# The last graph's elu on VectorE, and SyncE's flag load ahead of its waits, in a four-layer graph-attention kernel

## The chip, the cores and the metric

The kernel runs on one NeuronCore of one Trainium2 chip. The metric is the device time of one execution in microseconds (us), lower being better.

## What is computed

32 graphs of 256 nodes with 128 features pass through four residual layers, each on the rectified layer norm of x: a graph attention (0), an attention with four kinds of edges (1), a relational convolution (2), and a second graph attention whose output goes through an elu (3).

```python
h = jnp.maximum(_layernorm(x, axis=-1), 0.0)
x = x + _L0_gnn_ref(h, adj, L0_gnn_W, L0_gnn_a)
h = jnp.maximum(_layernorm(x, axis=-1), 0.0)
x = x + _L1_gnn_ref(h, adj, L1_gnn_a0, L1_gnn_a1, L1_gnn_a2, L1_gnn_a3)
h = jnp.maximum(_layernorm(x, axis=-1), 0.0)
x = x + _L2_gnn_ref(h, L2_gnn_adj, adj, L2_gnn_weight, L2_gnn_bias)
h = jnp.maximum(_layernorm(x, axis=-1), 0.0)
x = x + _L3_gnn_ref(h, adj, L3_gnn_W, L3_gnn_a)   # _L3_gnn_ref ends in jax.nn.elu(h_prime)
```

## The kernel before

The work is cut into 128 units, a layer of a graph each. `ORDER` lists them: layers 0 to 3 for the first 16 graphs, then for the other 16. A graph's 256 nodes lie as 2 x 128 on the partitions, so one tile of x is 128x256 f32. Each engine has its own hand-written program: `pipeline` steps through the units, and at each step calls a list of stages, each with its lag in units, so the list's order and the lags fix the order on each engine. Engines meet at semaphores alone.

What matters here is the end of layer 3 of the last graphs (g = 29, 30 and 31). TensorE puts numerators and sums in a bank (`put_o`). VectorE inverts the sums (`invert_sums`, L709 and L711). ScalarE (`elu_parts`, L566 and L567) makes for each half of the nodes exp(y) into `expy` and relu(y) into `relu_y`, four activations of 128x128 a graph, with the division in their `scale`. VectorE (`elu`, L735) makes min(exp, 1) + relu, which is elu + 1; the 1 was taken out of x before, through `bias_less_1`. Then x is added into `result`: by VectorE for odd graphs (`add_x`, L744), by GpSimd for even ones (`add_x_even`, L405). SyncE stores each result (L325), strictly in the order of the graphs.

Behind the last unit VectorE and TensorE reduce a flag (L756, L760, L1011, L762): it is over zero when the inputs are outside of what the fast path can compute, and then a general path in a loop recomputes everything. With these inputs it is zero. Every engine waits for the flag, loads it into a register and branches over the general path's code (L332 on SyncE, L416, L579, L766, L1034 on the others). The block ends with a meeting of all engines (L111): each drains, GpSimd gathers the signals and lets all go. SyncE alone waits before its flag load for all eight `stored` semaphores (L329).

Of the kernel before, what the change touches and what calls it, by code (L numbers as in the profile page):

```python
# [8 lines left out]
B, N, D = 32, 256, 128  # L9
P = 128  # L10
T = N // P
# [12 lines left out]


SLOTS = 8
BEHIND = 2
EARLY = 3
HS = 12
XS = 12  # L30
WIDE = 16
ROUNDS = B // SLOTS

ALL, ATTEND, GATS, NORMED, MULTI_REL, RGCN_REL = (0, 1, 2, 3), (0, 1, 3), (0, 3), (1, 2), (1,), (2,)
NOT_LAST, FIRST, LAST = (0, 1, 2), (0,), (3,)
# [14 lines left out]
def nth(layers, n):  # L50

    return COUNTS[layers][n]
# [21 lines left out]
def gat_slot(n):  # L74

    return (nth(GATS, n) - 1) % SLOTS

# [22 lines left out]
def gat_stack(nc, x, adj, w0, a0, m0, m1, m2, m3, w2, b2, w3, a3, out):  # L100
    f32, bf16, i32, u32 = mybir.dt.float32, mybir.dt.bfloat16, mybir.dt.int32, mybir.dt.uint32
    ALU = mybir.AluOpType
    ACT = mybir.ActivationFunctionType
# [7 lines left out]
    with ctx:  # L111
# [3 lines left out]
        def sem(name):  # L115
            return ctx.enter_context(nc.semaphore(name))
# [18 lines left out]
        x1 = sb("x1", [P, WIDE, T, D])  # L135
        edges = sb("edges", [P, SLOTS, T, N], i32)
        absent = sb("absent", [P, WIDE, T, N], bf16)

        h = sb("h", [P, HS, T, 1 + D])
        xb = sb("xb", [P, SLOTS, T, D])  # L140
        result = sb("result", [P, SLOTS, T, D])
        st = sb("st", [P, WIDE, T, 9])
# [4 lines left out]
        rinv = sb("rinv", [P, WIDE, T])  # L147

        hT = sb("hT", [P, 4, N])
        haT = sb("haT", [P, 4, N])  # L150
        val = sb("val", [P, SLOTS, T, D + 3])
        edgesT = sb("edgesT", [P, WIDE, T, N])
# [5 lines left out]
        relu_y = sb("relu_y", [P, 4, T, D])  # L158
        expy = sb("expy", [P, 4, T, D])
# [59 lines left out]
        def bank_o(n):  # L219
            return bank[O_BANK[n]][:, 0:T * (1 + D)].rearrange("p (t c) -> p t c", t=T)  # L220
# [4 lines left out]
        stored = [sem(f"stored{k}") for k in range(SLOTS)]  # L225
# [32 lines left out]
        sums_ready = sem("sums_ready")  # L258
        rinv_ready = sem("rinv_ready")
        elu_ready = sem("elu_ready")  # L260
        o_taken = sem("o_taken")
        xb_ready = sem("xb_ready")
        bias_ready = sem("bias_ready")
        result_ready = [sem("result_ready_even"), sem("result_ready_odd")]
# [28 lines left out]
        @block.sync  # L293
        def _(sp):

            def load_first(k):
                sp.dma_start(edges[:, k].rearrange("p t n -> p (t n)"), adj_v[k]).then_inc(edges_loaded[k], 16)

            for k in range(XS):
                sp.dma_start(xin[:, k].rearrange("p t d -> p (t d)"), x_v[k]).then_inc(x_loaded[k], 16)  # L300
                if 2 <= k <= SLOTS + 1:
                    load_first(k - 2)
                if k == 6:
                    sp.dma_start(w_gat[1][:, 0:D], w3).then_inc(gat_loaded[1], 16)
                    sp.dma_start(a_rows[1][:, :], a3.rearrange("(c p) o -> c (p o)", c=2)).then_inc(gat_loaded[1], 16)
            for r, m in enumerate((m0, m1, m2, m3)):
                sp.dma_start(a_rel[:, r:r + 1], m.rearrange("(p o) -> p o", o=1)).then_inc(loaded, 16)
            sp.dma_start(w_rel[:, :, :], w2.rearrange("r i o -> i r o")).then_inc(loaded, 16)
            sp.dma_start(bias[:, :], b2.rearrange("(o d) -> o d", o=1).to_broadcast([P, D])).then_inc(loaded, 16)

            def load_x(n, layer, g):
                if g + XS < B:
                    sp.wait_ge(o_taken, nth(NOT_LAST, n))
                    sp.dma_start(xin[:, g % XS].rearrange("p t d -> p (t d)"), x_v[g + XS]).then_inc(x_loaded[g % XS], 16)

            def load_edges(n, layer, g):
                k = g % SLOTS
                if g + SLOTS < B:
                    sp.wait_ge(absent_ready, nth(FIRST, n))
                    sp.dma_start(edges[:, k].rearrange("p t n -> p (t n)"), adj_v[g + SLOTS]).then_inc(edges_loaded[k], 16)  # L320

            def store(n, layer, g):
                k = g % SLOTS
                sp.wait_ge(result_ready[g % 2], (nth(LAST, n) + 1) // 2)
                sp.dma_start(out_v[g], result[:, k].rearrange("p t d -> p (t d)")).then_inc(stored[k], 16)  # L325

            pipeline([(load_x, SP_LAG, FIRST), (load_edges, SP_LAG, FIRST), (store, SP_LAG + 1, LAST)])
            for k in range(SLOTS):
                sp.wait_ge(stored[k], 16 * ROUNDS)  # L329

            sp.wait_ge(flag_ready, 1)
            with sp.If(sp.value_load(flag[0:1, 0:1], min_val=0, max_val=P) > 0):  # L332
                sp.sem_inc(g_step, 1)
                sp.sem_inc(g_stored, 16)
                with sp.Fori(0, B) as g:

                    sp.wait_ge(g_step, g * G + 1)
                    sp.dma_start(gx[:, :, :].rearrange("p t d -> p (t d)"), x_v[bass.ds(g, 1), :, :].rearrange("o p n -> (o p) n")).then_inc(g_loaded, 16)
                    sp.dma_start(gadj[:, :, :].rearrange("p t n -> p (t n)"), adj_v[bass.ds(g, 1), :, :].rearrange("o p n -> (o p) n")).then_inc(g_loaded, 16)
                    sp.wait_ge(g_step, g * G + G + 1)  # L340
                    sp.dma_start(out_v[bass.ds(g, 1), :, :].rearrange("o p n -> (o p) n"), gout[:, :, :].rearrange("p t d -> p (t d)")).then_inc(g_stored, 16)
                sp.wait_ge(g_stored, 16 * B + 16)

        @block.gpsimd
        def _(pool):
# [52 lines left out]

            def add_x_even(n, layer, g):
                k = g % SLOTS  # L400
                if g % 2 == 0:
                    pool.wait_ge(elu_ready, nth(LAST, n))
                    if g >= SLOTS:
                        pool.wait_ge(stored[k], 16 * (g // SLOTS))
                    pool.tensor_tensor(result[:, k], expy[:, (nth(LAST, n) - 1) % 4], x1[:, g % WIDE], ALU.add).then_inc(result_ready[0], 1)  # L405
# [21 lines left out]
        def _(act):  # L427
# [131 lines left out]
            def elu_parts(n, layer, g):  # L559
                k = g % SLOTS  # L560

                act.wait_ge(rinv_ready, nth(ATTEND, n))
                if nth(LAST, n) > 4:
                    act.wait_ge(result_ready[g % 2], (nth(LAST, n) - 3) // 2)
                for t in range(T):
                    act.activation(expy[:, (nth(LAST, n) - 1) % 4, t], bank_o(n)[:, t, 0:D], ACT.Exp, scale=rinv[:, n % WIDE, t:t + 1])  # L566
                    last = act.activation(relu_y[:, (nth(LAST, n) - 1) % 4, t], bank_o(n)[:, t, 0:D], ACT.Relu, scale=rinv[:, n % WIDE, t:t + 1])  # L567
                last.then_inc(y_ready, 1)

            pipeline([(upper_part, 6, MULTI_REL), (scale_v, 6, LAST), (take_hT, 4, FIRST),  # L570
# [29 lines left out]
        def _(dve):  # L600
# [130 lines left out]
            def elu(n, layer, g):  # L731
                k = g % SLOTS

                dve.wait_ge(y_ready, nth(LAST, n))
                dve.scalar_tensor_tensor(expy[:, (nth(LAST, n) - 1) % 4], expy[:, (nth(LAST, n) - 1) % 4], 1.0, relu_y[:, (nth(LAST, n) - 1) % 4], ALU.min,  # L735
                                         ALU.add).then_inc(elu_ready, 1)

            def add_x(n, layer, g):
                k = g % SLOTS
                if g % 2 == 1:  # L740
                    dve.wait_ge(elu_ready, nth(LAST, n))
                    if g >= SLOTS:
                        dve.wait_ge(stored[k], 16 * (g // SLOTS))
                    dve.tensor_tensor(result[:, k], expy[:, (nth(LAST, n) - 1) % 4], x1[:, g % WIDE], ALU.add).then_inc(result_ready[1], 1)  # L744
# [21 lines left out]
            with dve.If(dve.value_load(flag[0:1, 0:1], min_val=0, max_val=P) > 0):  # L766
                with dve.Fori(0, B) as g:
# [6 lines left out]
                    for t in range(T):  # L774
                        last = dve.tensor_scalar(cols(gabsent, t), adj_t[:, t], 0.0, -BIG, ALU.is_le, ALU.mult)
                    last.then_inc(g_step, 1)
                    for t in range(T):
                        last = dve.tensor_scalar(cols(grel, t), adj_t[:, t], 0.0, float(R + 1), ALU.max, ALU.min)
# [6 lines left out]
                    for layer in range(4):  # L785
                        turn(g, f"{layer}stats")
                        for t in range(T):
                            last = dve.bn_stats(gst[:, t, :], gx[:, t, :])
# [3 lines left out]
                        for t in range(T):  # L792
                            last = dve.bn_aggr(gmv[:, t, :], gst[:, t, :])
                        last.then_inc(g_step, 1)
                        turn(g, f"{layer}norm")
                        for t in range(T):
                            last = dve.tensor_scalar(gxn[:, t, :], gx[:, t, :], gmv[:, t, 0:1], grs[:, t:t + 1],
                                                     ALU.subtract, ALU.mult)
# [14 lines left out]
                        if layer == 2:  # L813
# [5 lines left out]
                            for t in range(T):  # L819
                                last = dve.tensor_tensor(gxb[:, t, :], gx[:, t, :], bias[:, :], ALU.add)  # L820
# [3 lines left out]
                        else:  # L824
# [4 lines left out]
                            for t in range(T):  # L829
                                last = dve.scalar_tensor_tensor(gx[:, t, :], ps_o[:, t, :], grinv[:, t:t + 1],  # L830
                                                                gx[:, t, :], ALU.mult, ALU.add)
# [3 lines left out]
                    for t in range(T):  # L835
                        last = dve.tensor_scalar(gy[:, t, :], ps_o[:, t, :], grinv[:, t:t + 1], None, ALU.mult)
# [267 lines left out]
```

## Time and profile before

| | |
|---|---|
| median of 3 runs | 287.89 us (287.56 to 288.56) |
| the profiled execution's own time | 288.05 us |
| its span, first to last instruction | 285.8 us |
| outside the span | 2.25 us |
| busy: TensorE, ScalarE, VectorE, GpSimd | 274.3, 255.0, 251.9, 234.1 us |
| granted TensorE clock over the span | 0.997 |

The busy times are averages over the whole execution. For a change at the very end the last ten microseconds count: which engine waits for which there, and who comes last to the meeting.

### The profile page before, as it was taken

The numbers are of one execution on the slowest core, as the hardware profiler recorded it, in microseconds if no ns is written. First come the engines' busy times: TensorE is split into PE (matmuls) and PEld (weight loads), VectorE is DVE, ScalarE is ACT, GpSimd is POOL, SyncE is SP. The second block draws the span as 40 slices with busy tenths as digits, with TensorE's granted clock in tenths as the row PEclk, the third lists the DMA queues.
The fourth block names the chain that finished last, engine by engine and source line by source line (L and its number), as shares of the span: only waits on it lengthen the run. The fifth ranks groups of instructions, "written<-read, shape, count | busy, mean of one in ns | idle before, by whom it ended". The sixth has DMA issues, their size and how long they took to land.

```text
span 285.8 us, 8113 instructions
## 1 busy us (share of the span) xinstructions
PE 274.3 (96%) x2252; PEld 257.9 (90%) x2252; DVE 251.9 (88%) x1217; ACT 255.0 (89%) x850; POOL 234.1 (82%) x376
## 2 busy tenths in 40 slices
PE   3999999999999999999999999999999999998991
PEld 2999998888889999999999999888889999998991
DVE  4889999988878887899999999998898888799985
ACT  5998988799998888999999999799999889796994
POOL 4998787777747999999999988887755899999722
PEclk9999999999999999999999999999999999999998
DMA  6946645400000000015333201000000000001213
GB/s 216 319 127 179 177 142 147 167 2 2 0 0 3 0 2 2 3 37 150 98 109 114 73 22 41 18 18 2 1 2 1 3 0 0 3 3 54 76 58 115
DMA packets 15414, 17.79 MB, mean 62 GB/s; under 512 B 2180, under 2 KB 11272, under 8 KB 15368
## 3 DMA queue, kind: packets, MB, share of 16 engines
q1 hardware_dynamic: 15220, 17.18, 19.9%
q8 instruction: 20, 0.33, 0.5%
q14 instruction: 26, 0.21, 0.3%
q10 hardware_dynamic: 148, 0.07, 0.1%
HBM read 13.05 MB, written 4.19 MB: 60 GB/s over the span
## 4 chain that ended last, share of the span: by engine, by line
PE 87%; DVE 8%; ACT 2%; issue 1%; POOL 0%; DVEq 0%; POOLq 0%
PE bank L1001 26%; PE bank L943 10%; PE bank L919 9%; PE bank L948 9%; PE bank L877 7%; PE bank L986 5%; PE bank L956 5%; PE bank L968 5%; PE bank L998 4%; PE bank L903 3%; PE bank L950 2%; DVE pT L699 2%; DVE expy L735 1%; PE bank L922 1%; DVE st L624 1%
## 5 line engine op out<-in xcount | busy, mean ns | idle before, releaser
L367 POOL TENSOR_TENSOR rs<-mv,minus_half 128x2 f32<-128x2 f32 x128 | 89.8, 702 | 35.5 <-DVE mv L635 35.0
L1001 PE MATMUL bank<-val,pT 128*128 128x129 f32 x512 | 74.6, 275 | 0.0
L1001 PEld LDWEIGHTS bank<-val,pT 128*128 128x128 f32 x512 | 67.3, 192 | 0.0
L384 POOL TENSOR_TENSOR h<-h,rs 128x256 f32<-128x256 f32 x93 | 58.2, 626 | 2.3
L699 DVE SCALAR_TENSOR_TENSOR pT<-bank,val,edgesT 128x256 f32<-128x256 f32 x128 | 55.0, 471 | 0.8 <-PE bank L956 0.7
L624 DVE BATCH_NORM_STATS2 st<-x 128x6 f32<-128x128 f32 x192 | 45.2, 276 | 0.0
L527 ACT ACTIVATE val<-bank,val 128x128 f32<-128x128 f32 x128 | 44.3, 437 | 0.1
L635 DVE BATCH_NORM_AGGREGATE mv<-st 128x2 f32<-128x9 f32 x256 | 33.5, 172 | 10.8 <-DVE st L624 1.0
L919 PE MATMUL bank<-w_gat,hT 128*128 128x131 f32 x256 | 40.3, 281 | 0.0
L376 POOL TENSOR_TENSOR h<-x,mv 128x256 f32<-128x256 f32 x64 | 40.1, 626 | 0.0
L877 PE MATMUL bank<-ident,h 128*128 128x128 f32 x192 | 38.0, 280 | 1.4 <-ACT hT L495 1.1
L948 PE MATMUL bank<-hT,haT 128*128 128x256 f32 x128 | 36.7, 382 | 0.0
L998 PE MATMUL bank<-ident,vsum 128*128 128x128 f32 x128 | 34.9, 273 | 0.0
L919 PEld LDWEIGHTS bank<-w_gat,hT 128*128 128x128 f32 x256 | 34.6, 195 | 0.0
L1001 PE MATMUL bank<-h,pT 128*128 128x129 f32 x256 | 34.0, 275 | 0.1
L550 ACT ACTIVATE prob<-neg_s,neg_max 128x256 f32<-128x256 f32 x64 | 29.4, 516 | 4.9 <-DVE neg_max L683 4.8
L943 PE MATMUL bank<-edgesT,h 128*128 128x256 f32 x128 | 32.9, 380 | 0.0
L1001 PEld LDWEIGHTS bank<-h,pT 128*128 128x128 f32 x256 | 31.3, 191 | 0.5 <-issue 0.3
L566 ACT ACTIVATE expy<-bank,rinv 128x128 f32<-128x128 f32 x64 | 29.2, 470 | 2.8 <-DVE rinv L711 2.7
L683 DVE CUSTOM_DVE_ANT_0 neg_s<-bank,upper 128x256 f32<-128x256 f32 x64 | 24.6, 421 | 7.0 <-ACT upper L545 6.5
L495 ACT ACTIVATE hT<-bank 128x256 f32<-128x256 f32 x64 | 27.9, 437 | 2.7 <-PE bank L877 2.3
L567 ACT ACTIVATE relu_y<-bank,rinv 128x128 f32<-128x128 f32 x64 | 29.5, 477 | 0.0
(87 smaller groups left out, 662.7 us busy)
## 6 DMA issues: line engine op xcount, KB each, us to landing
edges<-in_adj SPq DMA_DIRECT2D x32, 256.0 KB, 2.9
xin<-in_x SPq DMA_DIRECT2D x32, 128.0 KB, 2.6
out_x<-result SPq DMA_DIRECT2D x32, 128.0 KB, 1.7
w_rel<-in_L_gnn_weight SPq DMA_DIRECT2D x1, 256.0 KB, 2.8
w_gat<-in_L_gnn_W ACTq DMA_DIRECT2D x1, 64.0 KB
w_gat<-in_L_gnn_W SPq DMA_DIRECT2D x1, 64.0 KB
a_rel<-in_L_gnn_a SPq DMA_DIRECT2D x4, 0.5 KB, 3.0
bias<-in_L_gnn_bias SPq DMA_DIRECT2D x1, 64.0 KB, 3.3
```

What stands on the lines that cost most here:

```text
L367: pool.tensor_tensor(rs[:, n % WIDE], mv[:, n % WIDE, :, 1], minus_half[:, :], ALU.pow).then_inc(rs_ready, 1)
L376: pool.tensor_tensor(h[:, n % HS, :, 0:D], xin[:, g % XS] if layer == 0 else x1[:, g % WIDE], mv[:, n % WIDE, :, 0:1].to_broadcast([P, T, ...
L384: pool.tensor_tensor(h[:, n % HS, :, 0:D], h[:, n % HS, :, 0:D], rs[:, n % WIDE, :].rearrange("p (t o) -> p t o", o=1).to_broadcast([P, T, ...
L527: last = act.activation(val[:, n % SLOTS, t, 0:D], bank_v(n)[:, t, 0:D], ACT.Copy, scale=val[:, n % SLOTS, t, D:D + 1])
L624: last = dve.bn_stats(st[:, n % WIDE, t, 0:6], src[:, t])
L699: last = dve.scalar_tensor_tensor(pT[:, n % 4, u], bank_z(n)[:, 0], val[:, n % SLOTS, u, D + 2:D + 3], edgesT[:, g % WIDE, u], ALU.max, AL ...
L877: last = pe.transpose(bank_x(n)[:, t * P:(t + 1) * P], h[:, n % HS, t, 0:D], ident[:, :])
L919: last = pe.matmul(bank_v(n)[:, t], hT[:, n % 4, t * P:(t + 1) * P], w_gat[layer // 3][:, 0:D + 3], start=True, stop=True)
L943: last = pe.matmul(z[:, 0], h[:, n % HS, u, 0:D], edgesT[:, g % WIDE, u], start=(u == 0), stop=(u == T - 1))
L948: pe.matmul(z[:, t], haT[:, n % 4, t * P:(t + 1) * P], hT[:, n % 4], start=True, stop=False, skip_group_check=True)
L998: pe.matmul(bank_o(n)[:, t, 0:D], vsum[:, gat_slot(n):gat_slot(n) + 1].to_broadcast([P, P]), ident[:, :], start=True, stop=False, is_trans ...
L1001: last = pe.matmul(bank_o(n)[:, t], pT[:, n % 4, u, t * P:(t + 1) * P], values[:, u], start=(u == 0 and layer == 1), stop=(u == T - 1), sk ...
```

## The change

There are two edits. On SyncE the eight waits for the stores move from before the flag load to behind the branch; they are also put at the head of the general path, where they stand ahead of its loop. For the last graph (`LATE = 1`, g = 31) ScalarE makes only the two exponentials. VectorE then makes min(exp, 1) - 1 for the whole tile, the two halves of max(y, that), where y is read from the bank and divided by the sums on the way, and the sum with x and the 1 that is missing in x. Two semaphores, `late_elu` and `late_ready`, order these steps and the last store.

```diff
+LATE = 1
...
             def store(n, layer, g):
                 k = g % SLOTS
-                sp.wait_ge(result_ready[g % 2], (nth(LAST, n) + 1) // 2)
+                if g < B - LATE:
+                    sp.wait_ge(result_ready[g % 2], (nth(LAST, n) + 1) // 2)
+                else:
+                    sp.wait_ge(late_ready, g - (B - LATE) + 1)
                 sp.dma_start(out_v[g], result[:, k].rearrange("p t d -> p (t d)")).then_inc(stored[k], 16)
 
             pipeline([(load_x, SP_LAG, FIRST), (load_edges, SP_LAG, FIRST), (store, SP_LAG + 1, LAST)])
-            for k in range(SLOTS):
-                sp.wait_ge(stored[k], 16 * ROUNDS)
+            def all_stored():
+                for k in range(SLOTS):
+                    sp.wait_ge(stored[k], 16 * ROUNDS)
 
             sp.wait_ge(flag_ready, 1)
             with sp.If(sp.value_load(flag[0:1, 0:1], min_val=0, max_val=P) > 0):
+                all_stored()
                 sp.sem_inc(g_step, 1)
...
                 sp.wait_ge(g_stored, 16 * B + 16)
+            all_stored()
...
             def add_x_even(n, layer, g):
                 k = g % SLOTS
-                if g % 2 == 0:
+                if g % 2 == 0 and g < B - LATE:
...
                 for t in range(T):
-                    act.activation(expy[...], bank_o(n)[:, t, 0:D], ACT.Exp, scale=rinv[:, n % WIDE, t:t + 1])
-                    last = act.activation(relu_y[...], bank_o(n)[:, t, 0:D], ACT.Relu, scale=rinv[:, n % WIDE, t:t + 1])
+                    last = act.activation(expy[...], bank_o(n)[:, t, 0:D], ACT.Exp, scale=rinv[:, n % WIDE, t:t + 1])
+                    if g < B - LATE:
+                        last = act.activation(relu_y[...], bank_o(n)[:, t, 0:D], ACT.Relu, scale=rinv[:, n % WIDE, t:t + 1])
                 last.then_inc(y_ready, 1)
...
                 dve.wait_ge(y_ready, nth(LAST, n))
+                if g >= B - LATE:
+                    i = (nth(LAST, n) - 1) % 4
+                    dve.tensor_scalar(expy[:, i], expy[:, i], 1.0, -1.0, ALU.min, ALU.add).then_inc(elu_ready, 1)
+                    dve.wait_ge(elu_ready, nth(LAST, n))
+                    for t in range(T):
+                        last = dve.scalar_tensor_tensor(relu_y[:, i, t], bank_o(n)[:, t, 0:D], rinv[:, n % WIDE, t:t + 1],
+                                                        expy[:, i, t], ALU.mult, ALU.max)
+                    last.then_inc(late_elu, 1)
+                    return
...
             def add_x(n, layer, g):
                 k = g % SLOTS
-                if g % 2 == 1:
+                if g >= B - LATE:
+                    dve.wait_ge(late_elu, g - (B - LATE) + 1)
+                    dve.wait_ge(stored[k], 16 * (g // SLOTS))
+                    dve.scalar_tensor_tensor(result[:, k], relu_y[:, (nth(LAST, n) - 1) % 4], 1.0, x1[:, g % WIDE], ALU.add,
+                                             ALU.add).then_inc(late_ready, 1)
+                elif g % 2 == 1:
```

VectorE's program behind its last `invert_sums`, before (the two L735 of the first row are graphs 29 and 30, L744 is graph 29's; names in brackets are the semaphores waited for):

```order
L711 RECIPROCAL rinv<-sums 128x2 [waits sums_ready]
L735 SCALAR_TENSOR_TENSOR expy<-expy,relu_y 128x256 [waits y_ready] x2
L744 TENSOR_TENSOR result<-expy,x 128x256 [waits stored5,elu_ready]
L735 SCALAR_TENSOR_TENSOR expy<-expy,relu_y 128x256 [waits y_ready]
L744 TENSOR_TENSOR result<-expy,x 128x256 [waits stored7,elu_ready]
L756 TENSOR_SCALAR other<-neg_max 128x64 [waits scores_taken]
L760 TENSOR_REDUCE other_row<-other 128x1 [waits flag_step,wide_step]
L762 TENSOR_TENSOR flag<-bank,wide 1x1 [waits flag_step]
```

and with the change:

```order
L721 RECIPROCAL rinv<-sums 128x2 [waits sums_ready]
L754 SCALAR_TENSOR_TENSOR expy<-expy,relu_y 128x256 [waits y_ready] x2
L768 TENSOR_TENSOR result<-expy,x 128x256 [waits stored5,elu_ready]
L747 TENSOR_SCALAR expy<-expy 128x256 [waits y_ready]
L750 SCALAR_TENSOR_TENSOR relu_y<-bank,rinv,expy 128x128 [waits elu_ready]
L750 SCALAR_TENSOR_TENSOR relu_y<-bank,rinv,expy 128x128
L762 SCALAR_TENSOR_TENSOR result<-relu_y,x 128x256 [waits stored7,late_elu]
L780 TENSOR_SCALAR other<-neg_max 128x64 [waits scores_taken]
L784 TENSOR_REDUCE other_row<-other 128x1 [waits flag_step,wide_step]
L786 TENSOR_TENSOR flag<-bank,wide 1x1 [waits flag_step]
```

The two instructions of graph 31 have become four, and line numbers have moved (L735 is L754 now, L744 is L768, L756 is L780). SyncE's end, before:

```order
L325 DMA out_x<-result 128x256 [waits result_ready_odd]
L332 TENSOR_LOAD flag [waits stored5,stored4,stored6,stored3,stored7,stored2,flag_ready,stored1,stored0]
L332 ISA x2
L332 COMPARE_AND_BRANCH
L335 UNCONDITIONAL_BRANCH
```

and with the change:

```order
L331 DMA out_x<-result 128x256 [waits late_ready]
L339 TENSOR_LOAD flag [waits flag_ready]
L339 ISA x2
L339 COMPARE_AND_BRANCH
L343 UNCONDITIONAL_BRANCH [waits stored5,stored4,stored6,stored3,stored7,stored2,stored0,stored1]
...
L339 UNCONDITIONAL_BRANCH [waits general_stored]
L112 UNCONDITIONAL_BRANCH [waits stored4,stored5,stored3,stored6,stored2,stored7,stored1,stored0]
```

The flag load waits for the flag alone; the eight stores are waited for at the head of the general path and in front of the block's last branch.

## Rows read from the trace of the kernel before

**Rows 1.** The page: the span, and busy time by engine.

```profile
span 285.8 us, 8113 instructions
...
PE 274.3 (96%) x2252; PEld 257.9 (90%) x2252; DVE 251.9 (88%) x1217; ACT 255.0 (89%) x850; POOL 234.1 (82%) x376
```

**Rows 2.** Chain that ended last, late part: start us, us, what.

```profile
281.39 0.27 ACT relu_y L567
...
281.68 0.60 DVE expy L735
...
283.44 0.15 DVE flag L762
```

**Rows 3.** Timeline of the last graphs: start us, us, engine, line, op.

```profile
280.70 0.43 ACT L567 ACTIVATE relu_y<-bank,rinv 128x128 f32<-128x128 f32 x1
...
280.99 0.42 DVE L744 TENSOR_TENSOR result<-expy,x 128x256 f32<-128x256 f32 x1
281.15 0.83 POOL L405 TENSOR_TENSOR result<-expy,x 128x256 f32<-128x256 f32 x1 [0.78 <-DVE expy L735]
281.20 0.45 ACT L567 ACTIVATE relu_y<-bank,rinv 128x128 f32<-128x128 f32 x1
281.68 0.59 DVE L735 SCALAR_TENSOR_TENSOR expy<-expy,relu_y 128x256 f32<-128x256 f32 x1 [0.27 <-ACT relu_y L567]
282.30 0.42 DVE L744 TENSOR_TENSOR result<-expy,x 128x256 f32<-128x256 f32 x1
```

**Rows 4.** SyncE's waits before the branch, and the stores (L325).

```profile
L329 SPq EVENT_SEMAPHORE  x3: 28/28/28, 283.2 to 284.5; - x3
...
DMA to landing us min/median/max: 1.7/1.7/2.8
```

**Rows 5.** Flag load and branch of SyncE (L332) and VectorE (L766).

```profile
L332 SPq TENSOR_LOAD <-flag x1: 472/472/472, 284.6 to 284.6; - x1
...
L332 SPq COMPARE_BRANCH  x1: 50/50/50, 285.4 to 285.4; - x1
...
L766 DVEq TENSOR_LOAD <-flag x1: 536/536/536, 283.6 to 283.6; - x1
...
L766 DVEq COMPARE_BRANCH  x1: 72/72/72, 284.5 to 284.5; - x1
```

**Rows 6.** The meeting at the block's end, L111: durations ns, start us.

```profile
L111 DVEq DRAIN  x1: 45/45/45, 285.1 to 285.1; - x1
L111 SPq DRAIN  x1: 7/7/7, 285.6 to 285.6; - x1
L111 SPq EVENT_SEMAPHORE  x1: 17/17/17, 285.8 to 285.8; - x1
```

**Rows 7.** Timeline of VectorE and GpSimd at 257 us.

```profile
256.89 2.36 DVE L735 SCALAR_TENSOR_TENSOR expy<-expy,relu_y 128x256 f32<-128x256 f32 x1
...
257.10 0.73 POOL L405 TENSOR_TENSOR result<-expy,x 128x256 f32<-128x256 f32 x1
257.78 0.62 POOL L384 TENSOR_TENSOR h<-h,rs 128x256 f32<-128x256 f32 x1
258.34 0.62 POOL L376 TENSOR_TENSOR h<-x,mv 128x256 f32<-128x256 f32 x1
```

**Rows 8.** Timeline at 174 us: L649 beside GpSimd's L384.

```profile
173.98 0.61 POOL L384 TENSOR_TENSOR h<-h,rs 128x256 f32<-128x256 f32 x1
...
174.42 0.32 DVE L649 TENSOR_SCALAR h<-h 128x256 f32<-128x256 f32 x1
```

**Rows 9.** Timeline at 209 us: L649 beside GpSimd's L367.

```profile
209.46 0.29 DVE L649 TENSOR_SCALAR h<-h 128x256 f32<-128x256 f32 x1
...
209.07 0.72 POOL L367 TENSOR_TENSOR rs<-mv,minus_half 128x2 f32<-128x2 f32 x1 [0.71 <-DVE mv L635]
```

**Rows 10.** Durations of L649 (32 of them), and one pair of L727.

```profile
L649 DVE TENSOR_SCALAR h<-h x32: 247/254/318, 39.7 to 211.9; 128x256 f32<-128x256 f32 x32
...
185.71 0.61 DVE L727 SCALAR_TENSOR_TENSOR x<-bank,rinv,xin 128x128 f32<-128x128 f32 x2
```

More of the change, by code:

```diff
@@ L260, in gat_stack @@
         elu_ready = sem("elu_ready")
+        late_elu = sem("late_elu")
+        late_ready = sem("late_ready")
         o_taken = sem("o_taken")
@@ L565, in elu_parts @@
                 for t in range(T):
-                    act.activation(expy[:, (nth(LAST, n) - 1) % 4, t], bank_o(n)[:, t, 0:D], ACT.Exp, scale=rinv[:, n % WIDE, t:t + 1])
-                    last = act.activation(relu_y[:, (nth(LAST, n) - 1) % 4, t], bank_o(n)[:, t, 0:D], ACT.Relu, scale=rinv[:, n % WIDE, t:t + 1])
+                    last = act.activation(expy[:, (nth(LAST, n) - 1) % 4, t], bank_o(n)[:, t, 0:D], ACT.Exp, scale=rinv[:, n % WIDE, t:t + 1])
+                    if g < B - LATE:
+                        last = act.activation(relu_y[:, (nth(LAST, n) - 1) % 4, t], bank_o(n)[:, t, 0:D], ACT.Relu, scale=rinv[:, n % WIDE, t:t + 1])
                 last.then_inc(y_ready, 1)
```

## The prediction

> **What bounds the kernel now.** I read the page first. TensorE is busy for 274.3 of 285.8 us [rows 1], but the change touches nothing that TensorE waits for before its last product, so the span's mean is no guide; the last six microseconds are. The chain that ended last comes next [rows 2]: ScalarE's last relu (L567), VectorE's elu of graph 31 (L735), then the addition and the flag, ready at 283.44 + 0.15 = 283.6. Then the timeline of that stretch [rows 3]: the reader is to see that L735 waits for ScalarE, and that it takes 0.59 us though nothing but GpSimd's L405 runs beside it. Last the sequencers' own instructions, which the chain doesn't show. All engines but SyncE load the flag at 283.6. SyncE passes the last store at 284.5 [rows 4], loads the flag at 284.6 and branches at 285.4; VectorE branches at 284.5 [rows 5]. At the meeting VectorE drains at 285.1, SyncE at 285.6, and the last instruction stands at 285.8 [rows 6]. So **SyncE is last by 0.5 us**, and VectorE is next.
>
> **Edit 1, SyncE.** It removes nothing; it moves the load and branch (284.6 to 285.4, 0.8 us) [rows 5] from behind the stores to beside them. With the flag at 283.6, SyncE's load starts there, as those of the other engines did; its branch is at 284.4 and its waits start at about 284.6, just behind the landing (284.5). Behind the branch stand the eight waits, packed two to an instruction: four instructions at about 0.05 each, an estimate from the two that fit between the landing at 284.5 and the load at 284.6. SyncE then drains at 284.8. But the meeting now waits for VectorE at 285.1, so of SyncE's 0.8 us **0.5 is gained**. The rest lies under VectorE's branch.
>
> **Edit 2, ScalarE.** It drops two of four activations of graph 31. They started 0.25 us apart: the fourth ended at 281.20 + 0.45 = 281.65. Now the second exponential stands in the place of the relu at 280.70 and ends at 280.70 + 0.43 = 281.13 [rows 3]. That is 0.5 earlier for VectorE's wait, if VectorE can use it. VectorE's L744 for graph 29 runs from 280.99 to 281.41 anyway, so at most 0.3 of it is usable.
>
> **Edit 2, VectorE.** L735 and L744 of graph 31 become four instructions: a `tensor_scalar` of 128x256, two halves of 128x128 with an operand in the bank, and a sum of 128x256.
>
> The first is of the form of L649, 0.25 us in the median [rows 10]. The question is GpSimd's L405 for graph 30, which runs from 281.15 to 281.98 [rows 3], exactly where the new instruction wants to start. What the trace shows of such a meeting: L735 at 256.89 took 2.36 us beside three GpSimd additions in a row; the last of them ended at 258.34 + 0.62 = 258.96, and L735 at 259.25, 0.29 later [rows 7]. Graph 31's L735 ended at 282.27, again 0.29 after L405's end at 281.98 [rows 3]. So VectorE's instruction doesn't run slower, it is held until GpSimd is through. These have two operands in SBUF; L649 has one. It has one meeting of the kind: at 174.42 it ran for 0.32, and ended at 174.74, 0.15 after L384's end at 174.59 [rows 8]. Against it, beside L367, which reads only two elements a partition, it took 0.29 [rows 9]. L405 is a full-sized addition as L384 is, so I take the held case: the new instruction ends at 281.98 + 0.15 = **282.13**. The bounds are 281.66 (starting as soon as L744 is done at 281.41, and 0.25 long) and 282.27 (L735's 0.29 after L405).
>
> The Trainium skill (SBUF — State Buffer, section "Who interferes with whom") says that a two-port VectorE instruction and a GpSimd instruction share a port pair, and that whichever issues first blocks the other fully. By that rule the end is at 282.13; by the reading of a mere slowdown, as beside L367, it would be 281.41 + 0.29 = 281.70 and edit 2 would cost next to nothing. Rows 7 and 8 speak for the rule.
>
> A dependent instruction starts 0.03 behind the one before (282.27 to 282.30) [rows 3]. So the halves start at 282.16. They have the form of L727, whose pair takes 0.61 us [rows 10], as ever beside a busy GpSimd: 282.77. The sum starts at 282.80, has L744's size and takes 0.42: **283.22**, against 282.30 + 0.42 = 282.72 before. VectorE ends **0.50 later**, although ScalarE is done 0.5 earlier. All behind it moves along: flag at 284.1, last store issued 0.5 later and landed at 285.0, VectorE's drain at 285.6. SyncE: load at 284.1, branch at 284.9, waits from 285.1 (the store has landed at 285.0), drain at 285.3, under VectorE's 285.6.
>
> **Sum.** The last drain moves from SyncE's 285.6 to VectorE's 285.1 + 0.5 = 285.6: -0.5 + 0.5 = **0.0**. The span stays at 285.8 and the profiled execution at 288.05 us. That one stands 0.16 above the median of the three runs, so the forecast against the median is 287.9. The two semaphores and the renamed waits cost nothing I can see: they lie in the same instructions. The longest of the unknown terms, what an execution does outside of its span (2.25 us), I take as unchanged.
>
> **Rivals.**
> A, forecast: held by L405, no change, 287.9.
>
> B: the `tensor_scalar` slips in between L744 and L405. VectorE has it waiting from 281.13, and L405 itself looks as if it had waited for L744: it took 0.83 here and 0.73 at 257.10 [rows 3, 7]. If VectorE's next in line goes first, it ends at 281.41 + 0.25 = 281.66, the sum at 281.66 + 0.03 + 0.61 + 0.03 + 0.42 = 282.75, 0.0 later than before, and edit 1's 0.5 stays: 287.4. Against it: at 257 GpSimd's instructions followed each other without letting a waiting L735 in, so the one that stands first at the gap has it, and L405 asked before L744 was done. A gain above that would need VectorE's branch to get quicker as well; nothing moves there.
>
> C, slower: SyncE's jump. The general path that is jumped over is four instructions longer, and the code behind the branch is now needed at once. VectorE, which jumps over much more code, needs from 284.5 + 0.07 to 285.1, 0.5, from branch to drain; SyncE from 285.4 + 0.05 to 285.6, 0.15 [rows 5, 6]. If SyncE has to fetch its code, the price lies between VectorE's 0.5 and the 1.7 that a store takes from issue to landing [rows 4], the nearest row with a transfer. The end is then 284.95 + f + 0.2 for the four waits + 0.2 for the meeting: it decides from f = 0.45 on, passes 0.3% slower at f = 1.3, and is 287.05, 1.2 later, at 1.7: 289.1. Against it: SyncE's whole program is short, and it has jumped over nearly the same distance in 0.15.
>
> The Trainium skill (Runtime: NRT & Kernel Launch, "Instruction fetch mechanics") says that a taken branch whose target lies outside of the loaded window must fetch its page before going on. No row here shows such a fetch on SyncE; it would be rival C.
>
> **How the numbers follow.** 0.3% or 0.86 us is about what a measurement of this kernel can tell from no change. A gets 0.70, B 0.20, C 0.06, and 0.04 is for what I don't see. A and B both lie within 0.86 us of 287.89. The three runs spread over 1.0 us, so a median may be off by 0.3: from B it falls below 287.03 in a quarter of cases or so, from A hardly. Faster 0.08, within 0.84, slower 0.08 (C's upper half and the spread above A). The range takes in B with its spread and A's: 287.2 to 288.5; C above that is left out.
>
> **What would show it.** Right: in the changed trace the `tensor_scalar` of graph 31 lasts far over 0.25 us and ends 0.15 behind L405's end; VectorE's last sum ends near 283.2; SyncE's flag load starts together with the others'; VectorE, not SyncE, drains last, near 285.6. Wrong: the `tensor_scalar` takes 0.25 and GpSimd's L405 is the one that is stretched (B); or SyncE's gap from branch to waits is over 0.5 (C). A last store that lands late, 2.8 as the longest did [rows 4], would make SyncE last again in either kernel.

## The result, and the profile after

The changed kernel takes **288.93 us** in the median of nine runs (288.03 to 289.77), the kernel before 287.90 in nine runs beside it: 0.3% slower, ratio 1.0032 with a 95% interval of 1.0017 to 1.0047. The forecast was 287.9 with a range up to 288.5, so it was wrong, by 1.0 us. Yet the profiled execution (288.32 us) has a span of 285.8 us, the very span of before [rows 1]. The loss shows where no row of the first profile looked: outside of the span.

Inside it, the timeline answers to [rows 3] term by term (start us, us, engine, line, op; line numbers of the changed kernel, L768 was L744, L414 was L405):

```profile
280.85 0.42 DVE L768 TENSOR_TENSOR result<-expy,x 128x256 f32<-128x256 f32 x1
281.01 0.84 POOL L414 TENSOR_TENSOR result<-expy,x 128x256 f32<-128x256 f32 x1 [0.77 <-DVE expy L754]
281.19 0.81 DVE L747 TENSOR_SCALAR expy<-expy 128x256 f32<-128x256 f32 x1
...
282.03 0.61 DVE L750 SCALAR_TENSOR_TENSOR relu_y<-bank,rinv,expy 128x128 f32<-128x128 f32 x2
282.68 0.42 DVE L762 SCALAR_TENSOR_TENSOR result<-relu_y,x 128x256 f32<-128x256 f32 x1
...
283.82 0.15 DVE L786 TENSOR_TENSOR flag<-bank,wide 1x1 int32<-1x1 f32 x1 [0.28 <-PE bank L1035]
```

L747 is the new `tensor_scalar`: 0.81 us where the same form took 0.25 [rows 10]. It ends at 282.00, 0.15 behind GpSimd's end at 281.85, as L649 did at 174 us [rows 8]. The halves take 0.61, the last sum 0.42 and ends at 283.10. TensorE's last product came 0.13 earlier in this execution than in the one before, so that is 0.5 later than it was.

The flag loads, SyncE's branch and its waits (durations in ns, then first and last start in us), and the meeting:

```profile
L339 SPq TENSOR_LOAD <-flag x1: 466/466/466, 284.0 to 284.0; - x1
...
L339 SPq COMPARE_BRANCH  x1: 55/55/55, 284.8 to 284.8; - x1
...
L336 SPq EVENT_SEMAPHORE  x4: 17/28/28, 285.0 to 285.2; - x4
```

```profile
L112 SPq COMPARE_BRANCH  x1: 38/38/38, 285.3 to 285.3; - x1
L112 SPq DRAIN  x1: 7/7/7, 285.5 to 285.5; - x1
L112 DVEq DRAIN  x1: 46/46/46, 285.5 to 285.5; - x1
L112 SPq EVENT_SEMAPHORE  x1: 17/17/17, 285.7 to 285.7; - x1
```

SyncE (L339) loads at 284.0 with the others, branches at 284.8, passes its stores from 285.0 to 285.2 and drains at 285.5, just ahead of VectorE. In between stands a second branch of SyncE's (L112, 285.3), which its program before didn't have and which the forecast didn't count. The meeting ends at 285.7, where the forecast had 285.8.

What lies outside of the span is the time of a run less its span; every run lists both. For the kernel before, 35 runs that were taken beside the first four experiments have a median span of 285.5 and a median of **2.26** outside, none over 2.6 (of the 114 runs of before taken in all for this study one is, 3.09). Two more, of 359 and 477 us at a granted clock of 0.76 and 0.57, are left out throughout. The nine runs of the change have a median span of 285.7 and 2.49 to 2.54 outside four times, 3.23 to 3.37 five times: median **3.23**. So by the medians, which don't add up exactly, 0.2 of the loss is in the span and about 1.0 outside. The instructions that run outside aren't in the profile; that the time is lost at the close of a run, and not at its start, is inferred from the edits, which touch only the end. What the profile has of the close are fetches of instruction pages: the DMA view of the stretch from 285.3 to 287 of before, and from 285.7 to 287.4 of after (40 slices of 0.04 us; q8 and q14 are instruction queues):

```profile
DMA  0004009008000000000000000000000000000000
...
q8 instruction: 1, 0.02, 4.0%
q14 instruction: 2, 0.02, 3.2%
```

```profile
DMA  0060009000000004000000000000000000000000
...
q8 instruction: 1, 0.02, 3.5%
q14 instruction: 2, 0.02, 2.9%
```

The first row marks three fetches in each: 285.4, 285.6 and 285.7 before, 285.8, 286.0 and 286.4 after. The first of before comes 0.3 us ahead of the end of the meeting (285.8), the first of after behind it (285.7). The fetch on q8 is 16 KB. In the packet records of all fifteen traces of this study it starts 1.08 to 1.12 us behind the start of TensorE's branch over the general path (284.49 to 285.59 before, 284.87 to 285.98 after) and takes 1.0 to 1.5 us; that it is TensorE's is inferred from this constant distance.

### The profile page after: what moved, and what is told of

Same layout as the page of the kernel before. It is cut to its first block, busy times and chain, and to the rows that moved or that the text cites. A ratio compares the mean times of both kernels' runs of the same rounds, so it can differ in the third digit from the quotient of the medians.

```text
span 285.8 us, 8114 instructions
## 1 busy us (share of the span) xinstructions
PE 273.8 (96%) x2252; PEld 257.4 (90%) x2252; DVE 252.2 (88%) x1219; ACT 254.1 (89%) x848; POOL 234.0 (82%) x376
## 4 chain that ended last, share of the span: by engine, by line
PE 88%; DVE 6%; ACT 2%; DMA 2%; SPq 1%; issue 1%; DVEq 0%
PE bank L1025 28%; PE bank L972 10%; PE bank L967 10%; PE bank L943 9%; PE bank L901 7%; PE bank L1010 5%; PE bank L992 5%; PE bank L980 5%; PE bank L1022 4%; PE bank L974 2%; PE bank L927 2%; DMA edges<-in_adj 2%; DVE pT L709 2%; DVE expy L754 1%; PE bank L946 1%
## 5 line engine op out<-in xcount | busy, mean ns | idle before, releaser
L577 ACT ACTIVATE relu_y<-bank,rinv 128x128 f32<-128x128 f32 x62 | 28.6, 478 | 0.0
```

## The experiments

Thirteen kernels ran. The theories were: **CODE** (SyncE's code is longer), **ORDER** (SyncE's branch is no longer the last), **ELU** (the changed code of the two other engines), and later **MEETING TOO EARLY**: the end of a run waits for the pages that the taken branches ask for, so that a meeting which ends sooner only waits longer behind it.

### One part at a time

e1, SyncE's edit alone, is the change's diff on SyncE without the rest.

> SyncE's edit alone, the elu as before. All theories agree on the span: SyncE's 0.8 us of load and branch leave the end, VectorE drains last at 285.1, so the span falls by 0.5 to about 285.3. They differ on what lies outside of the span (time less span), which was 2.25 us in the profile before and is 2.5 or 3.3 in the nine runs of the change. Theory CODE: SyncE's longer code behind its flag load (waits twice over) makes the part outside longer: here too 2.5 to 3.3, time 287.8 to 288.6. Theory ORDER: it is that SyncE no longer branches last: the same here as under CODE. Theory ELU: the changed code of VectorE and ScalarE does it: here 2.25, time 287.4 (0.5 faster).

Measured: ratio 1.0018 (1.0002 to 1.0035), 288.40 against 287.84. Median span 285.1, as expected; outside 2.50 to 2.56 three times and 3.24 to 3.40 nine times. So an edit that shortens the span by 0.4 makes the run longer by 0.5, by an interval that only just leaves out no change; the part outside is clear of the noise. ELU falls as the only cause.

e2, the elu edit alone, has SyncE's waits where they were.

> The elu edit alone, SyncE as before. Span: VectorE's last sum is 0.5 later (the tensor_scalar held by GpSimd's addition), SyncE still branches last, so the span grows by 0.5 to 286.3. CODE and ORDER: outside stays at 2.25, time 288.4 (0.5 slower). ELU: outside 2.5 to 3.3, time 288.8 to 289.6.

Measured: ratio 1.0027 (1.0016 to 1.0038), 288.45. Median span 286.2, outside 2.23 in the median, one run of twelve over 3. The elu costs its 0.6 inside the span (0.7 by the medians), and nothing outside.

e3 adds code that isn't executed:

```diff
             with sp.If(sp.value_load(flag[0:1, 0:1], min_val=0, max_val=P) > 0):
+                for k in range(SLOTS):
+                    sp.wait_ge(stored[k], 16 * ROUNDS)
```

> The kernel before with the eight waits for the stores repeated at the head of SyncE's general path, which isn't executed: four more instructions of code, nothing else. Span 285.8 under all theories. CODE: outside grows from 2.25 to 2.5 to 3.3, time 288.2 to 288.9. ORDER and ELU: no change, 287.9.

Measured: ratio 0.9999 (0.9984 to 1.0015), outside 2.26 in the median of eleven runs. CODE falls.

e4 hides the load in another way, with the program at its old length:

```diff
-            for k in range(SLOTS):
-                sp.wait_ge(stored[k], 16 * ROUNDS)
-
             sp.wait_ge(flag_ready, 1)
-            with sp.If(sp.value_load(flag[0:1, 0:1], min_val=0, max_val=P) > 0):
+            wide_inputs = sp.value_load(flag[0:1, 0:1], min_val=0, max_val=P)
+            for k in range(SLOTS):
+                sp.wait_ge(stored[k], 16 * ROUNDS)
+            with sp.If(wide_inputs > 0):
```

> SyncE loads the flag, then waits for the stores, then branches: the load (0.47 us and what follows it) lies beside the stores, but no code is repeated, so the program has its old length and SyncE still branches last or nearly so. Span: SyncE branches right behind the landing at 284.5 and drains at 284.8, VectorE last at 285.1: 285.3 for the span. CODE: outside stays 2.25, time 287.4 (0.5 faster). ORDER: SyncE's branch is no longer the last event before the meeting, so outside 2.5 to 3.3, time 287.8 to 288.6.

Measured: ratio 1.0018 (0.9998 to 1.0039), 288.46; span 285.4, outside 2.48 to 2.60 six times and 3.24 to 3.33 six times. The span fell by 0.1 in the medians (profiled execution: 285.2), and CODE falls again. What e1, e4 and the change share is a meeting that ends 0.86 us behind TensorE's branch, where it was 1.28 in before, e2 and e3 (from each one's trace). In e4 SyncE's branch is the last one (284.46 against VectorE's 284.26) and the part outside is long all the same, which speaks against ORDER. And e4 has no second branch of SyncE's, so that isn't needed for the long part outside.

### Delays put back

e5 and e6 are e1 with SyncE's waits behind the branch written twice and three times:

```diff
             all_stored()
+            all_stored()
+            all_stored()      # e6 only
```

> SyncE's edit alone, with its eight waits written twice behind the branch: four more instructions, about 0.28 us of delay, all on semaphores that are already up. Found so far: where SyncE branches last (before, elu alone, dead waits) time less span is 2.0 to 2.6 us; where it doesn't (the change, SyncE alone, load first) it is 2.5 or 3.3. Theory MEETING TOO EARLY: instruction pages are fetched about 1.1 us behind each engine's branch (TensorE's 16 KB page always starts 1.09 us behind its branch), and a meeting that ends before that (0.86 us behind TensorE's branch in all three, 1.28 in the others) makes the closing code wait in a worse place. Here the meeting ends about 1.13 behind it: the first kernel for which the two cases mix; span 285.3, outside between, time at most that of SyncE alone (288.4). Theory ORDER (SyncE's branch not last): outside stays 2.5 or 3.3, so the time is 0.25 above SyncE alone, 288.6.

> As the one before with the waits written three times: 0.56 us of delay, the meeting ends about 1.4 us behind TensorE's branch, as in the kernel before. MEETING TOO EARLY: span 285.6, outside 2.25 again, time 287.8: a kernel with more waiting in it is 0.6 us faster than SyncE's edit alone. ORDER: span 285.6, outside 2.5 or 3.3, time 288.9.

Measured: e5 287.84, ratio 0.9996 (0.9979 to 1.0012), span 285.35, outside 2.22 to 2.58 nine times and 3.21 to 3.35 three times. e6 287.96, ratio 1.0000 (0.9984 to 1.0016), span 285.45, outside 1.94 to 2.57, no run over 3. Both have more waiting in them than e1, and their medians are 0.4 to 0.6 us lower. The intervals of the ratios overlap with that of e1, so the times alone don't settle it; the part outside does, with 9 of 12 runs over 3 in e1, 3 in e5 and none in e6. ORDER falls: in neither is SyncE's branch over the general path the last one. But in both SyncE drains last again, which leaves a rival, **LAST**: the closing part is short when SyncE is the last to drain.

e12 puts the same delay as e6 into the change itself.

> The changed kernel itself with SyncE's waits behind the branch written three times, about 0.56 us more of waiting. MEETING TOO EARLY (supported by the two delay kernels: 0.0 against the kernel before, where SyncE's edit alone was 0.5 slower): SyncE now drains last, about 0.5 later than VectorE did; span 286.2, but outside back to 2.25, and no run at 3.3: time 288.4, 0.5 faster than the change (288.93). If the 3.3 belongs to something else in the change: outside as before, time 289.4.

Measured: 288.67, ratio to before 1.0020 (1.0004 to 1.0036); span 286.3, outside 1.94 to 2.54, 2.49 in the median, no run over 3. The 3.3 is gone, and the median is 0.26 us under that of the change, half of what was expected. The two were not taken beside each other, and the 0.26 is within the spread of either; the part outside is what this run settles.

e13 is e1 with the delay on VectorE, so that the meeting is late and SyncE isn't last:

```diff
                     dve.tensor_tensor(gout[:, :, :], gw[:, :, :], gx[:, :, :], ALU.add).then_inc(g_step, 1)
+            for _ in range(2):
+                for k in range(SLOTS):
+                    dve.wait_ge(stored[k], 16 * ROUNDS)
```

> SyncE's edit alone, with eight wait instructions on semaphores that are already up on VectorE behind its branch: VectorE drains about 0.5 to 0.7 us later than in SyncE's edit alone and is last by far; SyncE isn't delayed. MEETING TOO EARLY: the meeting ends 1.4 us or more behind TensorE's branch, so time less span is 2.0 to 2.6 with no run at 3.3, span 285.7, time 287.9 to 288.1, 0.4 faster than without the delay. Rival LAST (the closing part is long when SyncE isn't the one that drains last): time less span stays 2.5 or 3.3, time 288.9 to 289.1.

Measured: 288.02, ratio 1.0005 (0.9989 to 1.0020); span 286.1, outside 1.88 to 2.03 in all twelve runs. The meeting's rows, of e1, then of e13:

```profile
L111 SPq DRAIN  x1: 7/7/7, 284.7 to 284.7; - x1
L111 DVEq DRAIN  x1: 46/46/46, 284.8 to 284.8; - x1
L111 SPq EVENT_SEMAPHORE  x1: 17/17/17, 285.0 to 285.0; - x1
```

```profile
L111 SPq DRAIN  x1: 7/7/7, 285.2 to 285.2; - x1
...
L111 DVEq DRAIN  x1: 17/17/17, 286.2 to 286.2; - x1
L111 SPq EVENT_SEMAPHORE  x1: 17/17/17, 286.4 to 286.4; - x1
```

VectorE drains 1.0 behind SyncE in e13, and the part outside is shorter than in any kernel before it. LAST falls. From e1 to e13 the span grows by 1.0 us and the median of the run falls by 0.4 us. The intervals of the two ratios overlap here too; that the run doesn't get longer by the 1.0 is clear.

### The flag earlier

If the end of a run hangs on the branches, they have to come earlier. e7 moves VectorE's part of the flag ahead of the last two elus, e8 is e7 with SyncE's edit:

```diff
             def elu(n, layer, g):
                 k = g % SLOTS
 
+                if g == B - 2:
+                    flag_rows()    # L756, L760
+                if g == B - 1:
+                    flag_sum()     # L762
                 dve.wait_ge(y_ready, nth(LAST, n))
```

> The kernel before with the flag's reductions moved ahead of the last two elus on VectorE, so that TensorE, ScalarE and GpSimd branch about 1 to 2 us earlier and VectorE 0.9 earlier; SyncE still waits for the stores first. The last store is at most 0.2 later, so the span is 285.6 to 286.0. If the end of a run is set by the page fetches behind the engines' branches (flag plus a constant), outside falls to 1.4 to 2.0 and the time to 287.0 to 287.5. If it is set by the meeting alone, outside stays 2.25 and the time 287.9 to 288.1.

> The early flag and SyncE's edit together, a version meant to beat both. SyncE loads the flag when it has issued the last store (283.1), branches at 283.9, passes the stores at 284.5 to 284.6 and drains at 284.8; VectorE drains at about 284.2, so the span is 285.0. The meeting ends 0.8 or more behind VectorE's branch (283.5) with its page at +1.2, and more than 1.1 behind TensorE's. MEETING TOO EARLY counted from TensorE: outside 2.25 or less, time 287.0 to 287.3. If SyncE's place alone decides (ORDER): outside 2.5 or 3.3, time 287.6 to 288.3.

Measured: e7 289.50, ratio 1.0051 (1.0035 to 1.0067); e8 288.70, 1.0018 (1.0001 to 1.0034). Outside fell to 1.76 to 1.91 and 1.84 to 1.93, as the theory says, but the spans rose to 287.6 and 286.85. The stores and the DMA view from 283.5 to 285.2 of e8:

```profile
DMA to landing us min/median/max: 1.7/1.7/3.4
```

```profile
DMA  6490009004789998966310000005000000000000
...
q1 hardware_dynamic: 168, 0.14, 25.1%
q8 instruction: 1, 0.02, 5.6%
```

The last store was issued at 283.06. Fifteen of its sixteen pieces had landed by 285.01, the sixteenth at 286.49. The q8 fetch ran from 283.79 to 285.32, beside the store's packets, and in the packet records the late packets start at 285.30. In e7 it is the same: fetch until 285.18, late packets from 285.16, the sixteenth piece at 286.35 against 285.30. One DMA engine's share of the store was late and the others' wasn't, so I read this as the engine that served the fetch as well: the page fetch, moved earlier, held the last store. It is inferred from the times; the rows don't name the engine.

e10 and e11 take the flag further ahead: `flag_rows` at the elu of graph 16, TensorE's product behind the last `put_v` (in unused columns of the same bank), `flag_sum` at the elu of graph 28. e11 has SyncE's edit too.

> The kernel before with the flag computed some 8 us before the end: VectorE's two reductions at the elu of graph 16, TensorE's product after the last put_v, VectorE's sum at the elu of graph 28. TensorE branches about 0.8 us behind its last product (near 280.7), so that its page fetch (1.1 behind the branch, about 1 us long) is over before the last store's packets, unlike in the early-flag kernels, where one of the store's sixteen pieces landed 1.4 us late beside that fetch. SyncE still waits for the stores first: span 285.5 to 285.8 as before, outside about 1.9 as there, time 287.4 to 287.6. Rival (the store still lands late, held by ScalarE's or VectorE's fetch): span over 286.5, time 288.4 or more.

> The same with SyncE's edit. The branch lies beside the last store, so SyncE drains 0.3 behind its landing, near 284.8; VectorE branches near 283.4 and drains at 284.0. Span 285.0, outside 1.9 to 2.2, time 286.9 to 287.3, the fastest of all. Rival as for the one before: a held store, span 286.5 to 287.

Measured: e10 288.35, ratio 1.0012 (0.9993 to 1.0032), span 286.55, outside 1.77. e11 **287.20**, ratio **0.9969** (0.9951 to 0.9986), span 285.4, outside 1.80: faster than both kernels, by 0.9 us against the kernel before. TensorE's page is fetched from 281.7 to 283.1 in e11's trace, ahead of the last store, which was issued at 283.59 and landed at 285.5. The store before that one, issued at 282.49 beside the fetch, took 2.5 us to land instead of 1.7. Its meeting:

```profile
L111 PEldq DRAIN  x1: 72/72/72, 281.0 to 281.0; - x1
L111 ACTq DRAIN  x1: 81/81/81, 282.1 to 282.1; - x1
L111 POOLq DRAIN  x1: 45/45/45, 282.7 to 282.7; - x1
L111 DVEq DRAIN  x1: 45/45/45, 284.3 to 284.3; - x1
...
L111 SPq DRAIN  x1: 7/7/7, 285.8 to 285.8; - x1
L111 SPq EVENT_SEMAPHORE  x1: 17/17/17, 285.9 to 285.9; - x1
```

TensorE, ScalarE and GpSimd drain 3 to 5 us ahead of SyncE, which is last because of the store alone. e10 missed its expected 287.4 to 287.6. Its last store was not held (1.7 us to land), but in its profiled execution TensorE's last product starts 1.25 later than in before (0.5 later in e11), and the last store is issued as much later (283.99 against 282.75). Why TensorE is later there, no run shows. Between e10 and e11 SyncE's edit is worth 1.15 us, where it cost 0.5 on the kernel before. In the traces the meeting ends 1.32 behind the last landing in e10 and 0.43 in e11, so about 0.9 of it is the load and the branch; the rest is not accounted for.

### The held instruction

e9 is e2 with GpSimd's addition for graph 30 replaced by a memset of one column, so it leaves out the result of graph 30.

> The elu edit alone, and GpSimd's addition of x for graph 30 left out: a one-column memset, which reads nothing, stands in its place. Leaves out: the result of graph 30. Theory HELD (VectorE's tensor_scalar of graph 31 waits for GpSimd's addition, which took 0.81 us in the change's profile against 0.25 in the median of L649): here it takes 0.25 to 0.29, and VectorE's last sum ends 0.5 to 0.6 earlier relative to TensorE's last product than in the elu kernel. Rival (the form itself, in place and with two operations, is slow): it takes 0.8 here too.

Measured, in a single execution: 287.55 us. VectorE's timeline of e9:

```profile
280.32 0.42 DVE L768 TENSOR_TENSOR result<-expy,x 128x256 f32<-128x256 f32 x1
280.65 0.28 DVE L747 TENSOR_SCALAR expy<-expy 128x256 f32<-128x256 f32 x1
280.97 0.61 DVE L750 SCALAR_TENSOR_TENSOR relu_y<-bank,rinv,expy 128x128 f32<-128x128 f32 x2
281.62 0.42 DVE L762 SCALAR_TENSOR_TENSOR result<-relu_y,x 128x256 f32<-128x256 f32 x1
```

The `tensor_scalar` takes 0.28 instead of 0.81, and the last sum ends 3.13 behind the start of TensorE's last product, against 3.65 in e2: 0.52 less. The form is not slow; GpSimd's addition held it.

### The distance, in one table

| kernel | meeting's end behind the start of TensorE's branch, in its trace | outside the span, median (runs over 3) |
|---|---|---|
| e4, e1, change | 0.86 to 0.87 | 2.92 (6 of 12), 3.30 (9 of 12), 3.23 (5 of 9) |
| e5 | 1.00 | 2.51 (3 of 12) |
| e6, e12 | 1.25 | 2.41, 2.49 (0 of 24) |
| before, e3, e2 | 1.28 to 1.29 | 2.26 (1 of 114), 2.26 (0 of 11), 2.23 (1 of 12) |
| e13 | 1.81 | 1.94 (0 of 12) |
| e7, e8, e10, e11 | 4.2 to 5.7 | 1.88, 1.90, 1.77, 1.81 (0 of 48) |

A rival is the distance from the last store's landing: the meeting ends 0.9 behind it in e4, e1 and the change, and 1.3 in before, e6 and e12. It falls with e8 and e11, where that distance is 0.43 and the part outside 1.8 to 1.9.

The distance alone doesn't say why executions of one kernel differ. The packet records go further: the fifteen profiled executions fall into groups by where the q8 fetch lands, which is the distance and the fetch's own length together (spans are taken to 0.01 here, where the runs list them to 0.1).

| q8 fetch lands behind the span's end, us | traces | that execution's time outside, us |
|---|---|---|
| 1.6 to 3.6 ahead of the end | e7, e8, e10, e11 | 1.79 to 1.88 |
| 0.23 to 0.77 | e13, e3, e6 | 1.98 to 1.99 |
| 0.86, 0.92 | before, e2 | 2.23, 2.26 |
| 1.11 to 1.22 | e5, e12, change, e9 | 2.42 to 2.54 |
| 1.40, 1.55 | e4, e1 | 3.28, 3.37 |

So the change's profiled execution has the distance of e1 (0.86) but a fetch of 0.96 us where e1's took 1.37, and it stays at 2.54 us outside. The two executions over 3 are also the only ones with fetches 3 us behind the span's end, here in e1 from 287.5 to 289.2:

```profile
DMA  0000000000000580000000000000000000000000
...
q14 instruction: 2, 0.02, 3.5%
```

Whether these late fetches are a cause of the 3.3 or only come with it, no run shows.

## Why the prediction was wrong

**Edit 2 was right.** The held `tensor_scalar` was forecast to end 0.15 behind GpSimd's addition and did, to 0.01. The pair took the 0.61, the sum the 0.42; VectorE ended 0.5 later, and e2 shows it as 0.6 of the whole. e9 shows that the hold is the cause. Rival B fell: GpSimd's waiting addition had the gap before VectorE's next instruction.

**Edit 1 was right inside the span and wrong as a gain.** SyncE's load and branch left the end as forecast, VectorE drained last, and e1's span is 0.4 shorter. The step that failed is the sentence that followed from it, that of SyncE's 0.8 us "0.5 is gained", together with "what an execution does outside of its span (2.25 us), I take as unchanged". It is not a constant. It grew from 2.26 to 3.30 in e1 and to 3.23 in the change, which took back the 0.5 and another 0.5. The sum that would have been right is -0.5 + 0.5 + 1.0 for SyncE, VectorE and the part outside: +1.0. That the elu's 0.5 delay of VectorE didn't lengthen the distance between branch and meeting follows from the same rows: the branches wait for VectorE's flag, so they moved with it.

**Rival C was near the cause, but in the wrong place.** It looked for a page fetch behind SyncE's branch, in the span. SyncE's gap from branch to its waits was 0.2 in the change, and e3's longer code did nothing. The Trainium skill (Runtime: NRT & Kernel Launch, "Instruction fetch mechanics") says that a taken branch out of the window must fetch a page before execution goes on. No row shows which pages were loaded, so the rule itself isn't tested here. What the traces show is that the engines went on to the meeting before the fetch started: in before TensorE branches at 284.49 and drains at 284.91, and the fetch starts at 285.59. That the code behind the meeting bears the wait is inferred from the two tables.

**The figures on the spread were too kind.** The range ended at 288.5, with A's spread, because only C could pass it and C was left out; an unknown of 2.25 us that no row bounded should have widened it.

What stays open: why the part outside takes steps (about 2.0, 2.25, 2.5 and 3.3, and nothing between 2.6 and 3.2 in the kernels with a short distance), why one fetch takes 1.0 us and another 1.5, and whether the pages are what the closing code waits for. All kernels fit the distance and all fifteen traces the fetch's landing, and no row shows the wait itself.

## What to carry to other kernels

A span that gets shorter is no gain until the run gets shorter: compare time less span for both kernels before crediting work removed from behind the last barrier. Where engines end with a taken branch over a long body, bring the branch forward, since here TensorE's page fetch starts 1.1 us behind it, and keep that fetch clear of the last store. On VectorE, an addition with two SBUF operands, or a `tensor_scalar` of 128x256 f32 with one, should not be placed beside a full-sized GpSimd addition: in these traces each waited until that was through.

## What the hardware showed that was not expected

The end of a run goes with how long before the last barrier the engines branched: 2.9 to 3.3 us outside of the span at 0.86 us, 2.26 at 1.28, 1.94 at 1.8, and 1.8 to 1.9 at 4 us or more. Adding SyncE's waits once more to e1 (e5) took the runs over 3 from 9 of 12 to 3, and with them the median of the run from 288.40 to 287.84.

An instruction page fetch of 16 KB can hold a part of a store: one sixteenth of a 128 KB store landed 1.5 us behind the other fifteen in e8 and 1.05 behind in e7, inferred from late packets that start within 0.02 us of the fetch's end.

GpSimd's addition holds a single-operand `tensor_scalar` of VectorE as fully as one with two operands: end 0.15 behind GpSimd's end at 174 us, in the change and in e12's trace (281.90 against 281.75).
